# Loads and stores cut in halves and tied to TensorE's stages, in a cross-attention and LoRA-mixture kernel

## The reference, cut to what matters

```python
qh = softmax(heads(layernorm(x)), over the 64 channels of a head)
kh = softmax(heads(ctx), over the 2048 positions);  vh = heads(ctx)
x  = x + qh @ (kh^T @ vh)                       # per head, 64 x 64 in the middle
flat   = layernorm(x).reshape(-1, 2048)
gates  = softmax(top 2 of 4 of (flat @ router_w.T))
mid    = flat @ A[e].T  (4 experts of rank 16)
x      = x + sum_e gates[e] * (mid[e] @ B[e].T) * 4
```

## Time and profile before

| | |
|---|---|
| median of three runs | 496.2 us (488.34 to 496.86) |
| the profiled execution | 493.56 us |
| its span, first to last instruction | 491.8 us |
| mean granted TensorE clock | 0.944 |
| busy: TensorE matmuls, VectorE, GpSimd, ScalarE | 404.7, 416.6, 358.9, 241.4 us |
| DMA: moved, mean rate | 137.95 MB, 281 GB/s |

### The profile page before, as it was taken

One profiled execution on the slowest core, in us unless ns is written; L12 is line 12 of the kernel. 1 busy time (PEld: TensorE's weight loads), 2 busy tenths in 40 slices (PEclk: granted clock), 3 DMA queues, 4 the chain that ended last, 5 costly groups with the idle time before them and its releaser, 6 DMA issues.

```text
span 491.8 us, 22601 instructions
## 1 busy us (share of the span) xinstructions
PE 404.7 (82%) x9960; PEld 346.6 (70%) x9960; DVE 416.6 (85%) x1109; ACT 241.4 (49%) x340; POOL 358.9 (73%) x341
## 2 busy tenths in 40 slices
PE   5477877979988898879888898979889887989764
PEld 5466766868777677768776777868677676878543
DVE  2598888989998999899987999989999998976652
ACT  1155556545555455555555356545655556564100
POOL 1369997878888787878877787887878786985200
PEclk9568999999999998999998999999999999999955
DMA  8987686587979797787977698887879795532243
GB/s 332 427 329 291 253 315 259 205 311 285 345 263 344 273 390 255 263 332 297 379 279 296 260 331 336 286 316 274 320 282 367 267 384 213 195 152 91 112 188 128
DMA packets 24689, 137.95 MB, mean 281 GB/s; under 512 B 2192, under 2 KB 4368, under 8 KB 12176
## 3 DMA queue, kind: packets, MB, share of 16 engines
q1 hardware_dynamic: 24592, 136.51, 73.5%
HBM read 102.95 MB, written 33.55 MB: 278 GB/s over the span
## 4 chain that ended last, share of the span: by engine, by line
PE 39%; DVE 35%; issue 16%; DMA 4%; POOL 3%; ACT 2%; SPq 1%; DVEq 0%; POOLq 0%
DVE y_sb L631 9%; PE num_ps L367 8%; DVE max_n L566 8%; PE kv_ps L348 7%; PE kv_ps L398 6%; PE delta_ps L431 6%; PE raw_ps L384 6%; DVE bn_parts L582 4%; DMA sq_a<-in_bt_dram 4%; PE delta_ps L432 3%; DVE rden L619 3%; DVE attnT L622 3%; POOL y_sb L287 2%; DVE rz L611 1%; DVE midT L722 1%
## 5 line engine op out<-in xcount | busy, mean ns | idle before, releaser
L287 POOL TENSOR_TENSOR y_sb<-attnT,y_sb 128x512 f32<-128x512 f32 x128 | 164.6, 1286 | 78.6 <-DVE attnT L622 77.3
L275 POOL TENSOR_TENSOR ek_sb<-ctx_sb,kmax_row 128x512 f32<-128x512 f32 x128 | 167.5, 1311 | 15.7 <-ACT kmax_row L464 15.7
L431 PE MATMUL delta_ps<-midT,b_hi 128*128 128x256 f32 x256 | 83.3, 346 | 38.2 <-DVE y_sb L631 37.0
L367 PE MATMUL num_ps<-kv_sb,x_sb 64*64 64x65 f32 x4096 | 94.5, 228 | 8.6 <-issue 7.5
L631 DVE TENSOR_TENSOR y_sb<-delta_ps,y_sb 128x512 f32<-128x512 f32 x128 | 87.5, 683 | 15.8 <-PE delta_ps L432 15.3
L348 PE MATMUL kv_ps<-ctx_sb,ek_sb 128*64 128x65 f32 x2048 | 94.0, 234 | 7.0 <-issue 4.2
L566 DVE TENSOR_REDUCE max_n<-ctx_sb 128x32 f32<-128x512 f32 x128 | 86.4, 677 | 10.8 <-DMA ctx_sb<-in_ctxt_dram 10.4
L622 DVE TENSOR_TENSOR attnT<-num_ps,rden 128x512 f32<-128x512 f32 x128 | 88.5, 691 | 4.6 <-DVE rden L619 0.2
L348 PEld LDWEIGHTS kv_ps<-ctx_sb,ek_sb 128*64 128x64 f32 x2048 | 75.1, 140 | 22.9 <-issue 8.8
L367 PEld LDWEIGHTS num_ps<-kv_sb,x_sb 64*64 64x64 f32 x4096 | 75.2, 137 | 22.6 <-issue 15.0
L384 PE MATMUL raw_ps<-w_sb,y_sb 128*64 128x69 f32 x2048 | 86.6, 225 | 4.4 <-issue 4.4
(11 more groups left out here) (55 smaller groups left out, 324.7 us busy)
## 6 DMA issues: line engine op xcount, KB each, us to landing
ctx_sb<-in_ctxt_dram SPq DMA_DIRECT2D x32, 1040.0 KB, 5.6
x_sb<-in_x_dram SPq DMA_DIRECT2D x32, 1024.0 KB, 8.0
y_sb<-in_xt_dram SPq DMA_DIRECT2D x32, 1024.0 KB, 9.7
out_dram<-y_sb SPq DMA_DIRECT2D x30, 1024.0 KB, 5.9
out_dram<-y_sb SPq DMA_DIRECT2D x8, 256.0 KB, 2.1
sq_a<-in_bt_dram SPq DMA_DIRECT2D x1, 1024.0 KB, 18.5
w_sb<-in_wt_dram SPq DMA_DIRECT2D x1, 552.0 KB, 10.8
cst<-in_consts_dram SPq DMA_DIRECT2D x1, 145.0 KB, 2.3
```

The lines of the kernel that those rows point to most:

```text
L275: pool.tensor_tensor(ek_sb[:, t % 2, chunks(g), :].rearrange("p (a b) c -> p a b c", b=2), ctx_sb[:, t % 4, 2 * g:2 * g + 2, 1:P + 1, :].r ...
L287: pool.tensor_tensor(y, attnT[:, g, :], y, ALU.add).then_inc(x1_made, 1)
L367: mm = pe.matmul(num_ps[n, h, j * (DH + 1):(j + 1) * (DH + 1)], x_sb[d, t % 4, c * P + half * DH:c * P + (half + 1) * DH], kv_sb[d, t % 2, ...
L431: pe.matmul(to, b_hi[:, j * P:(j + 1) * P], midT[:, p % 2, :], start=True, stop=False)
```

## The change

The three loads of a tile are cut in two halves each (`PIECES = 2`): ctx by its first and last 8 chunks of 128 positions, x and y by columns. A store is now half of the columns of one tile (512 KB) in place of half of the columns of a pair (1024 KB). A half is contiguous over 4160 bytes (ctx) or 4096 bytes (x, y) in each partition, where the whole was 8320 and 8192; a store's pieces are 4096 bytes both before and after. SP's loop takes two quarters a step. In each step, in this order: one store (at q = 26, 28, 30, 32 + 8p; it waits for `raw_done` of quarter q - 2 and for `out_made`), half a load of x (waits for `num_done` of quarter q - 1), half a load of y (waits for `raw_done` of quarter q - 1, and for the stores of the slot), half a load of ctx (waits for `kv_done` of quarter q + 1). A half of x or ctx waits only for the quarters that read that half. Those who read a tile still wait for both halves. The last pair is stored as before. The twelve loads ahead of the loop become twenty-one, in the same order. Nothing is changed in what an engine computes, or in its order.

```diff
@@ -121,7 +121,8 @@
         ctx_landed = [sem(f"ctx_landed{i}") for i in range(4)]
         x_landed = [sem(f"x_landed{i}") for i in range(4)]
         y_landed = [sem(f"y_landed{i}") for i in range(8)]
-        out_stored = [sem(f"out_stored{i}") for i in range(4)]
+        out_stored = [sem(f"out_stored{i}") for i in range(8)]
+        last_stored = sem("last_stored")
         cst_landed = sem("cst_landed")
         w_landed = sem("w_landed")
         b_landed = sem("b_landed")
@@ -212,57 +213,85 @@
 
         @block.sync
         def _(sp):
-            def load_ctx(t):
-                sp.dma_start(ctx_sb[:, t % 4, :, :, :].rearrange("p a c b -> p a (c b)"),
-                             ctxt[t].rearrange("p a c b -> p a (c b)")).then_inc(ctx_landed[t % 4], 16)
-
-            def load_x(t):
-                sp.dma_start(x_sb[:, t % 4, :], x_rows[t * P:(t + 1) * P, :]).then_inc(x_landed[t % 4], 16)
-
-            def load_y(t):
-                sp.dma_start(y_sb[:, t % 8, :, :], xt[t]).then_inc(y_landed[t % 8], 16)
-
-            def store(p, h, parts=1):
-                n = 8 // parts
-                for i in range(parts):
-                    sp.wait_ge(out_made, 8 * p + 4 * h + 4 * (i + 1) // parts)
-                    c = slice(8 * h + n * i, 8 * h + n * (i + 1))
-                    sp.dma_start(out[2 * p:2 * p + 2, :, c, :].rearrange("t p j c -> p t (j c)"),
-                                 y_sb[:, pair_slots(p), c, :].rearrange("p t j c -> p t (j c)")
-                                 ).then_inc(out_stored[p % 4], 16)
+            PIECES = 2
+            CP = NCH // 2 // PIECES
+            XW = N // PIECES
+            YC = NCH // PIECES
+
+            def load_ctx(t, k):
+                c = slice(k * CP, (k + 1) * CP)
+                sp.dma_start(ctx_sb[:, t % 4, c, :, :].rearrange("p a c b -> p a (c b)"),
+                             ctxt[t][:, c, :, :].rearrange("p a c b -> p a (c b)")).then_inc(ctx_landed[t % 4], 16)
+
+            def load_x(t, k):
+                c = slice(k * XW, (k + 1) * XW)
+                sp.dma_start(x_sb[:, t % 4, c], x_rows[t * P:(t + 1) * P, c]).then_inc(x_landed[t % 4], 16)
+
+            def load_y(t, k):
+                c = slice(k * YC, (k + 1) * YC)
+                sp.dma_start(y_sb[:, t % 8, c, :], xt[t][:, c, :]).then_inc(y_landed[t % 8], 16)
+
+            def store(t, k):
+                c = slice(k * YC, (k + 1) * YC)
+                sp.dma_start(out[t, :, c, :].rearrange("p j c -> p (j c)"),
+                             y_sb[:, t % 8, c, :].rearrange("p j c -> p (j c)")).then_inc(out_stored[t % 8], 16)
+
+            def store_last(i):
+                c = slice(2 * i, 2 * i + 2)
+                sp.dma_start(out[NT - 2:NT, :, c, :].rearrange("t p j c -> p t (j c)"),
+                             y_sb[:, pair_slots(NP - 1), c, :].rearrange("p t j c -> p t (j c)")
+                             ).then_inc(last_stored, 16)
+
+            def whole(load, t):
+                for k in range(PIECES):
+                    load(t, k)
+
+            def quarters_done(q, offset):
+
+                return min(q - offset + 1, 4 * NT)
 
             sp.dma_start(cst[:], consts).then_inc(cst_landed, 16)
-            load_ctx(0)
-            load_x(0)
-            load_ctx(1)
+            whole(load_ctx, 0)
+            whole(load_x, 0)
+            whole(load_ctx, 1)
             sp.dma_start(w_sb[:], wt).then_inc(w_landed, 16)
-            load_x(1)
-            load_ctx(2)
-            load_y(0)
+            whole(load_x, 1)
+            whole(load_ctx, 2)
+            whole(load_y, 0)
             sp.dma_start(b_rows, bt).then_inc(b_landed, 16)
-            load_y(1)
-            load_x(2)
-            load_ctx(3)
-            for q in range(0, LAST + 3):
-                p, i = delta_at(q - 1)
-                if p is not None and i in (3, 7):
-                    store(p, i // 4, 1 if p < NP - 1 else 4)
-                t, g = tile_at(q, -12)
-                if t is not None and t >= 4 and g == 0:
-                    sp.wait_ge(kv_done, 4 * (t - 4) + 4)
-                    load_ctx(t)
-                t, g = tile_at(q, -8)
-                if t is not None and t >= 3 and g == 0:
-                    after(sp, num_done, 4 * (t - 4) + 4)
-                    load_x(t)
-                t, g = tile_at(q, -1)
-                if t is not None and t >= 2 and g == 0:
+            whole(load_y, 1)
+            whole(load_x, 2)
+            whole(load_ctx, 3)
+            STEP = 4 // PIECES
+            for q in range(0, 4 * NT + 28, STEP):
+                last = q + STEP - 1
+                p, r = divmod(q - 26, 8)
+                if 0 <= p < NP - 1:
+                    t, k = 2 * p + r // STEP % 2, r // (2 * STEP)
+                    after(sp, raw_done, quarters_done(q - 1, 7))
+                    sp.wait_ge(out_made, 8 * p + 8 // PIECES * (k + 1))
+                    store(t, k)
+                t, r = divmod(q + 10, 4)
+                if 3 <= t < NT:
+                    after(sp, num_done, 4 * (t - 4) + r + STEP)
+                    load_x(t, r // STEP)
+                t, r = divmod(q, 4)
+                if 2 <= t < NT:
+                    after(sp, raw_done, quarters_done(q, 7))
                     if t >= 8:
-                        old = (t - 8) // 2
-                        sp.wait_ge(out_stored[old % 4], 32 * (old // 4 + 1))
-                    load_y(t)
-            for p in range(NP - 4, NP):
-                sp.wait_ge(out_stored[p % 4], 32 * (p // 4) + (32 if p < NP - 1 else 128))
+                        sp.wait_ge(out_stored[t % 8], 16 * PIECES * (t // 8))
+                    load_y(t, r // STEP)
+                t, r = divmod(q + 16, 4)
+                if t < NT:
+                    sp.wait_ge(kv_done, 4 * (t - 4) + r + STEP)
+                    load_ctx(t, r // STEP)
+            for i in range(8):
+                sp.wait_ge(out_made, 8 * (NP - 1) + i + 1)
+                store_last(i)
+            for k in range(8):
+                uses = len(range(k, NT - 2, 8))
+                sp.wait_ge(out_stored[k], 16 * PIECES * uses)
+            sp.wait_ge(last_stored, 16 * 8)
 
         @block.gpsimd
         def _(pool):
@@ -281,7 +310,7 @@
                 if t is None:
                     return
                 if g == 0:
-                    pool.wait_ge(y_landed[t % 8], 16 * (t // 8 + 1))
+                    pool.wait_ge(y_landed[t % 8], 32 * (t // 8 + 1))
                 pool.wait_ge(attn_made, 4 * t + g + 1)
                 y = y_sb[:, t % 8, chunks(g), :].rearrange("p j c -> p (j c)")
                 pool.tensor_tensor(y, attnT[:, g, :], y, ALU.add).then_inc(x1_made, 1)
@@ -560,7 +589,7 @@
                 if t is None:
                     return
                 if g == 0:
-                    dve.wait_ge(ctx_landed[t % 4], 16 * (t // 4 + 1))
+                    dve.wait_ge(ctx_landed[t % 4], 32 * (t // 4 + 1))
                     after(dve, maxT_done, t - 1)
                 c = slice(g * 32, (g + 1) * 32)
                 dve.tensor_reduce(max_n[:, t % 2, c], ctx_sb[:, t % 4, :, 1 + g * 32:33 + g * 32, :].rearrange("p a c b -> p c a b"), AX.XY,
@@ -578,7 +607,7 @@
                 if t is None:
                     return
                 if g == 0:
-                    dve.wait_ge(x_landed[t % 4], 16 * (t // 4 + 1))
+                    dve.wait_ge(x_landed[t % 4], 32 * (t // 4 + 1))
                 dve.bn_stats(bn_parts[:, t % 4, g, :], x_sb[:, t % 4, cols(g)]).then_inc(bn_parts_made, 1)
 
             def ln1(q):
```

## The result

The changed kernel takes 512.38 us in the median of four runs (508.15 to 515.62), the kernel before 493.58 (four runs, 488.34 to 496.86): ratio 1.0459, interval 1.0319 to 1.0599. It is 4.6% slower where 3% faster was forecast. The profiled execution took 511.76 us, 18.2 more than before's.

A forecast was written before the change was run, and what follows sets the result against it. VectorE's 25.53 us a pair was taken as the floor, with TensorE's stalls on late instruction blocks on top; 493.56 - 16 (steady part) + 0.5 (start) = 478 us, range 470 to 494.

The forecast's parts named there:

- What bounds the kernel: Steady part: VectorE needs 25.53 us a pair; TensorE stalls on late instruction blocks, costing 24.6 us with clock.
- halves and stages, steady part: Steady loop: spread halves take 85%, 21 us, of stalls from TensorE; VectorE then limits the gain to 16 us.
- The cover: TensorE's instruction stream: work in hand lasts the first 4 to 5 us while a late block is awaited.
- The peak of 1.67 MB: Steady part after the change: most data ever outstanding, 4.2 us of DMA work in place of 7.
- What a pair takes without stalls: Steady part: 26.4 us a pair in place of 27.55, 16 us over 14 pairs' worth of time.
- The 3 us that I put down to stalls for the clock: TensorE's matmuls run at 1.2 GHz for a while behind two long stalls: 1.2 to 1.5 us each.
- Added waits: SP's new waits for `raw_done` and y's later second half: costed at nothing, with 11 us left before y is wanted.
- more DMAs at the start: Extra DMAs ahead of the loop delay B's rows: +0.5 us, ends 0 and 5; steady part nothing.
- The slower one: Rival "Even traffic hits every block": regular bursts meet four blocks in five, TensorE covers only 2 us; 506 us, chance 0.05.
- VectorE holds the pace: Rival: stalls go, but pairs still take 27.2 to 27.4 us; 489 us, chance 0.11.
- the stalls stay: Rival: instruction blocks don't queue behind outstanding data or are late for their own reason; 494 us, chance 0.18.
- The page against halves: Skill's rule of 1 MiB or more per DMA: about 2 us fixed cost per half, sum 490 if nothing overlapped.

The follow-up runs named there:

- light kernels: Kernel before and changed kernel, each with three quarters of the traffic left out: 484.49 and 489.34 us (before; 0.987), 482.03 and 491.44 us (changed).
- experiments 5 and 7: 5: kernel before with whole transfers spread, one per quarter, 492.02 us, 0.9927; 7: changed kernel with its four halves issued apart, 493.28 us, 0.9978.
- Experiment 8: 96 DMAs of 8 KB added, one ahead of each load: to the kernel before, 1.0254; to the kernel with whole transfers spread over quarters, 0.9940.

## Why the prediction was wrong

- **What bounds the kernel: right.** VectorE's floor with TensorE's stalls on top. The light kernels show that the data's DMAs make the stalls, and the packets that land 1.2 to 1.6 us before the end of every one show that late blocks of TensorE's instructions are what it waits for.
- **The step that failed is "halves and stages, steady part", and in it the rule that a block of instructions waits for all that is outstanding, with 4 to 5 us covered.** Bytes issued less bytes moved, taken through the traces from 60 to 440 us, are at most 3.7 MB in the kernel before and 2.5 MB in the changed one. The peak did fall, and the stalls rose from 21.6 to 38.0 us where 85% should have gone. In experiments 5 and 7 the peak is 2.0 MB, with 17.5 and 21.4 us of stalls. Experiment 8 adds under 1% of bytes and twelve more us of waits, and nothing where transfers are spread. Bytes aren't without effect: the more is outstanding, the longer a block waits (correlation 0.6 before, 0.7 after). But they don't give the wait.
- **The cover was too long as well.** It was read from one stall after 7 us of calculated backlog. I now take the end of the previous 256 instructions as the moment at which a block is asked for. This is an estimate; for it speaks that in the light kernels the packet starts 0.7 and 0.8 us later in the median. From there the packet starts 2.1 us later before and 2.9 after, and over 3 us later 23 times before and 33 times after. Of those, 17 and 27 are stalls, and only 5 and 1 stalls follow a shorter wait. So about 3 us are covered, not 4 to 5.
- **The peak of 1.67 MB was too low.** It took four halves to be moved at 390 to 400 GB/s and through after 5.3 us. That was the rate of 1 MB transfers already under way. In 44 fours of the changed kernel, from 92 to 404 us, the first 5 us run at 209 to 369 GB/s, 281 in the median; the 216 above is one of the slowest. When the next four starts, 0 to 1.0 MB of the last is still outstanding, 0.4 in the median, so the bunches do run into one another. The count of the backlog before was off too: the trace has 3.5 MB outstanding at 206.0, not 2.8. I also wrote down the doubt, "two bursts 1.1 us apart", and priced it at nothing.
- **What a pair takes without stalls: right.** 26.4 us were taken, 26.54 to 26.59 are shown by nine windows of a light kernel. But the whole gain to be had was some 6 us (0 to 13), not 16: two pairs of the light kernel take 28.0 and 28.2 us at a mean clock of 0.94 without a stall. The 3 us that I put down to stalls for the clock may then not be theirs; the light kernel works on stale tiles, so this isn't shown for the real data.
- **Added waits, more DMAs at the start: right.** Nothing waits for y, and SP's waits are free as far as two runs each tell (484.49 and 489.34 us, 482.03 and 491.44). Half a y landed in 7.3 us, though, and not in 4 to 6. The chain of the changed kernel, in order of time, begins so:

```profile
8.21 15.71 DMA sq_a<-in_bt_dram
```

  B's rows landed at 23.92 us in place of 23.34: 0.6 us, where 0.5 was taken.
- **The rivals.** The slower one named the right wait (short cover, more blocks hit, 32 us of stall and 506 us; it became 38.0 and 512.38) at a chance of 0.05. Its sum gives 501, 24.6 off and 32 on; the other 5 us had no row behind them. And it was for a reason that the runs refute: the traffic of experiments 5 and 7 is at least as even, and costs nothing. The bunch was the cause, and not the loss of idle stretches. "VectorE holds the pace" fell with the stalls' increase, and so did "the stalls stay".
- **The page against halves.** The Trainium skill ("DMA: Bandwidth & Descriptors", section "Rules for kernel authors") wants 1 MiB or more in a DMA for the most bandwidth. The traces agree as to the DMA engines' time: the data's packets took 0.735 of 491.8 us before, 361 us, and 403 in the changed kernel. But with the halves apart it is still 394, and that kernel is as fast as the one before, so this isn't what the change cost.
- **The page on turns.** By the Trainium skill ("DMA: Bandwidth & Descriptors", section "Queues, rings and completion order") a queue waits for packets of another, not for all that is outstanding. That agrees with a peak that falls while the stalls rise. It isn't enough for "the stalls stay": why spacing and 96 tiny DMAs decide how long a block waits, no run here shows.

## What to carry to other kernels

An engine with a long instruction stream depends on the DMA engines although no tile says so: look for its stalls on "issue" in the middle of like instructions, see whether a packet of an instruction queue lands just before each of them ends, and set them beside what the DMA queue has issued just before. Between 512 KB and 1 MB, spacing mattered more here than size: tie each transfer to a stage of its own, and don't let several waits on one queue come true at the same moment, which is what happens to steps written one after another behind a common wait. Take a transfer rate for a bunch only from a stretch in which one was started.

## What the runs showed of the hardware that was not expected

- Loads of 64 partitions each, two for a tile, ran at 229 GB/s with the DMA engines at a share of 0.92; whole ones at 307 with 0.82. That cost 28.7% of the time.
- 96 DMAs of 8 KB cost 2.5% when each stands ahead of a load in a bunch, and nothing in spread traffic. The data's packets have the same share of the DMA engines' time in the first as without them, 0.735.
- All 389 stalls of TensorE on "issue", in seventeen traces, end 1.0 to 1.7 us after a packet of 16,384 bytes of the instruction queue has landed, a multiple of 256 instructions apart but for 8 that are off by two.
- Where three half loads and a half store are issued within 1.5 to 4.3 us, the first 5 us run at 281 GB/s in the median (209 to 369).
- The mean granted clock of TensorE was 0.94 in four windows, from 158.76 to 268.10 us, of a light kernel whose only two stalls, of 0.8 and 0.9 us, end at 73.36 and 85.45 us.
- Why a bunch of DMAs delays TensorE's instructions more than the same bytes spread stays open.
